# A graph layer on one core: four more units of eight tiles, the left-edge check in another bank, and 14 slots for gathered rows

## The reference

```python
hs = h[src]; hd = h[dst]; e = concatenate([hs, hd], axis=1)
a_k = exp(relu(e @ W_att_k + b_att_k))              # k = 1, 2, 3
att_k = segment_sum(a_k, dst)
avg_a = (a1 / att1[dst] + a2 / att2[dst] + a3 / att3[dst]) / 3.0
m = avg_a * relu(relu(relu(hs @ W_msg_1 + b_msg_1) @ W_msg_2 + b_msg_2) @ W_msg_3 + b_msg_3)
h_neigh = segment_sum(m, dst) / maximum(deg, 1.0)
out = relu(concatenate([h, h_neigh], axis=1) @ W_c1 + b_c1) @ W_c2 + b_c2
x = layernorm(x + out)
```

## Time and profile before

| | us |
|---|---|
| three runs | 770.85, 774.49, 776.41 (median 774.49) |
| the profiled execution | 772.04 |
| its span, first to last instruction | 767.9 |
| granted TensorE clock over the span, share of full | 0.864 |
| PE, DVE, ACT, POOL busy | 651.9, 593.9, 486.6, 553.2 |

### The profile page before, as it was taken

How to read it: one execution, slowest core, us unless ns; L and a number is a source line. 1 busy time by engine, 2 the same in 40 slices (tenths; PEclk the granted TensorE clock), 3 DMA queues, 4 the chain that set the end, 5 groups by cost and what they waited for, 6 DMA issues and landing times.

```text
span 767.9 us, 17623 instructions
## 1 busy us (share of the span) xinstructions
PE 651.9 (85%) x5388; PEld 535.7 (70%) x5388; DVE 593.9 (77%) x1881; ACT 486.6 (63%) x1128; POOL 553.2 (72%) x576
## 2 busy tenths in 40 slices
PE   8962679898879957789999999999988888888785
PEld 5752457765656633469999999999977777777664
DVE  4883577989777969877888888888765778777776
ACT  5554776877665536557777777777565555655563
POOL 7677777777777775467777777777777777777760
PEclk9985597879797776659999999999989788989797
DMA  7984353433883323223333333333352444445431
GB/s 224 258 207 105 67 80 82 97 81 79 77 71 86 67 59 88 46 56 72 82 79 81 79 81 80 82 82 79 76 137 65 107 131 107 118 105 136 101 95 34
DMA packets 81572, 73.70 MB, mean 96 GB/s; under 512 B 34056, under 2 KB 65472, under 8 KB 81472
## 3 DMA queue, kind: packets, MB, share of 16 engines
q0 software_dynamic: 18112, 37.94, 25.3%
q1 hardware_dynamic: 63072, 34.43, 16.8%
q10 hardware_dynamic: 288, 0.13, 0.1%
HBM read 62.91 MB, written 9.52 MB: 94 GB/s over the span
## 4 chain that ended last, share of the span: by engine, by line
PE 43%; POOL 22%; DVE 13%; issue 12%; ACT 6%; DMA 2%; DVEq 1%; SPq 0%; ACTq 0%
POOL work L1428 22%; PE bank L1660 15%; PE bank L1615 9%; PE bank L1641 3%; PE bank L1621 3%; DVE counts L1940 3%; DVE acc L1925 2%; DVE acc L2128 2%; ACT acc L1777 2%; PE bank L646 2%; PE bank L667 2%; PE bank L1567 1%; DMA work<-message_table,src_t 1%; PE bank L655 1%; PE bank L1572 1%
## 5 line engine op out<-in xcount | busy, mean ns | idle before, releaser
L1428 POOL DMA_INDIRECT work<-message_table,src_t x526 | 511.8, 973 | 178.4 <-issue 155.9
L1615 PE MATMUL bank<-work 128*128 128x144 f32 (+7 forms) x1132 | 175.8, 310 | 24.0 <-DVE acc L2128 23.9
L1615 PEld LDWEIGHTS bank<-work 128*128 128x128 f32 x1132 | 163.6, 220 | 33.8 <-issue 19.3
L1803 ACT COPY work<-bank 128x192 f32<-128x192 f32 (+5 forms) x120 | 36.0, 300 | 183.1 <-DVE work L2078 181.0
L2128 DVE TENSOR_TENSOR acc<-acc,bank 128x192 f32 (+7 forms) x283 | 85.9, 303 | 27.0 <-issue 4.4
L1660 PE MATMUL bank<-shared,acc 128*128 128x129 f32 (+1 forms) x784 | 95.6, 275 | 0.0
L2109 DVE TENSOR_TENSOR work<-bank,work 128x576 f32<-128x576 f32 (+5 forms) x120 | 83.5, 696 | 12.5
L1660 PEld LDWEIGHTS bank<-shared,acc 128*128 128x128 f32 (+1 forms) x784 | 91.5, 192 | 0.0
L1641 PE MATMUL bank<-acc 128*128 128x294 bf16 (+3 forms) x240 | 64.4, 406 | 29.6 <-ACT acc L1782 20.9
L1940 DVE TENSOR_TENSOR counts<-counts,bank 128x294 f32 (+3 forms) x120 | 68.9, 574 | 11.4 <-issue 7.5
L1641 PEld LDWEIGHTS bank<-acc 128*128 128x128 bf16 x240 | 23.1, 113 | 69.5 <-ACT acc L1782 36.5
(11 more groups left out here) (188 smaller groups left out, 999.6 us busy)
## 6 DMA issues: line engine op xcount, KB each, us to landing
work<-message_table,src_t POOLq DMA_INDIRECT x526
side<-near_nodes SPq DMA_DIRECT2D x97, 48.0 KB
side<-logit_parts SPq DMA_DIRECT2D x283, 0.8 KB
message_table<-work SPq DMA_DIRECT2D x12, 262.0 KB, 4.5
work<-message_table SPq DMA_DIRECT2D x48, 65.5 KB, 1.8
work<-in_x_t SPq DMA_DIRECT2D x12, 256.0 KB, 4.2
counts<-in_x SPq DMA_DIRECT2D x11, 256.0 KB, 3.4
logits_or_x<-in_x_t SPq DMA_DIRECT2D x11, 256.0 KB
```

Of the source, the lines that this page charges most:

```text
L1428: pool.indirect_dma_start(out=rows_of(n)[:, t, :], out_offset=None, in_=table[:, :], in_offset=bass.IndirectOffsetOnAxis(ap=src_t[:, h, g: ...
L1615: pe.matmul(sums[:, at:at + HEADS * w], rows_here[:, t, 0:P], wt_of(i)[:, t, :], start=h == 0, stop=h == TILES - 1)
```

## The change

`LONG` becomes 26, so units 22 to 25 have eight tiles too: 26 long and 90 short units, 116 in all. The first pass has a ring of 14 slots (`WIDER`) for its first 98 places and of 12 after that; slots 12 and 13 lie in the spare part of plane 3 of `acc`. `FINAL_EVERY` becomes (3, 2): the wide ones begin in steps 81, 83, 86, 88, ..., 101, 103, the next two in 107 and 111. The left-edge check's transpose comes a step later, in step 21, into bank 3, and waits for the early layers' last rows (`s_erow`); the waits of and for the counting bank are gone. Four semaphores are merged with others, whose counts are raised to match.

```diff
-LONG = 22
+LONG = 26
-RING = 12
+RING, WIDER = 12, 14
+WIDER_TO = 7 * WIDER
...
+        more_slots = []
+        for plane, at_slots in ((HEADS, at_spare),):
+            view, _ = spare_area(plane, at_slots, TWO * CHUNK * ROW)
+            more_slots.append(view.rearrange("p (t f) -> p t f", f=ROW))
...
-        LEFT_STEPS, LEFT_PE, LEFT_END = (0, 17, 18, 19), 20, 21
+        LEFT_STEPS, LEFT_PE, LEFT_END = (0, 17, 18, 19), 21, 22
...
-        LEFT_BANK = COUNT_BANKS[LEFT_NEXT % FOUR]
...
-        FINAL_EVERY, FINAL_STEPS = (3, 3), 8
+        FINAL_EVERY, FINAL_STEPS = (3, 2), 8
...
+            def gath_slot(p):
+
+                if not first:
+                    return p % RING
+                return p % WIDER if p < WIDER_TO else (p - WIDER_TO) % RING
+
+            def slot_user(p):
+
+                back = WIDER if first and p < WIDER_TO + RING else RING
+                return max((n for n in range(n_units) if place[n] <= p - back), default=-1)
+
+            def slot_rows(p):
+
+                j = gath_slot(p)
+                if j < RING:
+                    return gath, j * CHUNK
+                return more_slots[(j - RING) // TWO], (j - RING) % TWO * CHUNK
...
+            left_bank = EARLY_BANK if first else SIDE_BANKS[0]
...
                     for n, u in enumerate(order):
-                        if taken(n, RING) >= 0:
-                            pool.wait_ge(s_sum, groups_to(taken(n, RING)))
+                        before = slot_user(place[n] + places[n] - 1)
+                        if before >= 0:
+                            pool.wait_ge(s_sum, groups_to(before))
...
-                                if item == LEFT_NEXT:
-                                    pe.wait_ge(s_left, len(LEFT_STEPS) + 1)
...
                         if i == LEFT_PE:
                             pe.wait_ge(s_left, len(LEFT_STEPS))
                             if first:
-                                pe.wait_ge(s_cadd, LEFT_FREE)
-                            pe.transpose(bank[LEFT_BANK][0:1, 0:P], least[:, :], ident[:, :]).then_inc(s_least, 1)
+                                pe.wait_ge(s_erow, EARLY)
+                            pe.transpose(bank[left_bank][0:1, 0:P], least[:, :], ident[:, :]).then_inc(s_least, 1)
...
-                            act.activation(here, here, ACT.Abs, bias=less_col[0:WIN, 0:1]).then_inc(s_gap, 1)
-                            act.wait_ge(s_gap, before + h + 1)
+                            act.activation(here, here, ACT.Abs, bias=less_col[0:WIN, 0:1]).then_inc(s_hot, 1)
+                            act.wait_ge(s_hot, TWO * (before + h) + 1)
```

More of the change, by code:

```diff
@@ L699, in gnn_program @@
         assert columns_most + UNIT * PARTS <= 512
-        LEFT_STEPS, LEFT_PE, LEFT_END = (0, 17, 18, 19), 20, 21
-        assert LEFT_END < HOT_AT - 4 and LEFT_PE * PAIRS < n_hot
+        LEFT_STEPS, LEFT_PE, LEFT_END = (0, 17, 18, 19), 21, 22
+        assert LEFT_END < HOT_AT - 4 and EARLY_EVERY * EARLY < LEFT_PE
         ONES_AT = max(LEFT_END, early_units[-1])
@@ L799, in gnn_program @@
         s_least = sem("s_least")
-        s_gath = [sem(f"s_gath{j}") for j in range(RING)]
+        s_gath = [sem(f"s_gath{j}") for j in range(WIDER)]
         s_fill = sem("s_fill")
@@ L1271, in taken @@
                 return sum(at < place[i] + places[i] - ring for at in place) - 1
+            def gath_slot(p):
[10 more added lines that the diff above has]
+                return more_slots[(j - RING) // TWO], (j - RING) % TWO * CHUNK
+            assert not first or WIDER_TO <= place[hot_end - TWO]
             def uses(i, ring):
@@ L1311, in early_rows @@
             def early_rows(k):
-                at = (place[early_units[k]] + 1) % RING * CHUNK
-                return gath[:, at:at + CHUNK, 0:P]
+                ring, at = slot_rows(place[early_units[k]] + 1)
+                return ring[:, at:at + CHUNK, 0:P]
             def q_bank(i):
@@ L1333, in rows_of @@
             def rows_of(i):
-                at = place[i] % RING * CHUNK
-                return gath[:, at:at + n_tiles(i), :]
+                ring, at = slot_rows(place[i])
+                return ring[:, at:at + n_tiles(i), :]
             def tiles_at(i, h):
@@ L1345, in rows_landed @@
                         continue
[L1346 removed]
+                    slot = gath_slot(place[i] + h)
                     eng.wait_ge(s_gath[slot], 16 * sum(tiles_at(n, k) for n in range(i + 1) for k in range(places[n])
[L1348 removed]
+                                                       if gath_slot(place[n] + k) == slot))
             def near_of(i):
@@ L1430, in _ @@
                                     in_offset=bass.IndirectOffsetOnAxis(ap=src_t[:, h, g:g + 1], axis=0),
-                                ).then_inc(s_gath[(place[n] + t // CHUNK) % RING], 16)
+                                ).then_inc(s_gath[gath_slot(place[n] + t // CHUNK)], 16)
                     for n in range(n_units - RING, n_units):
@@ L1854, in _ @@
                             for k, a, b in spare_pieces[i - hot_end::ZERO_STEPS]:
-                                act.copy(acc[:, k, a:b], zero_col[:, 0:1].to_broadcast([P, b - a])).then_inc(s_spare, 1)
+                                act.copy(acc[:, k, a:b], zero_col[:, 0:1].to_broadcast([P, b - a])).then_inc(s_zero, 1)
                         for c, step in final_steps(i):
@@ L2062, in another_pass @@
                         dve.wait_ge(s_least, 1)
-                        dve.tensor_reduce(least_all[:, :], bank[LEFT_BANK][0:1, 0:P], AX,
+                        dve.tensor_reduce(least_all[:, :], bank[left_bank][0:1, 0:P], AX,
                                           ALU.min).then_inc(s_left, 1)
@@ L2089, in rows_early @@
                         dve.wait_ge(s_e3, k + 1)
-                        before = max((n for n in range(n_units) if place[n] <= place[early_units[k]] + 1 - RING),
-                                     default=-1)
+                        before = slot_user(place[early_units[k]] + 1)
                         if before >= 0:
@@ L2119, in add_sums @@
                         if first and i == hot_end + ZERO_STEPS:
-                            dve.wait_ge(s_spare, len(spare_pieces))
+                            dve.wait_ge(s_zero, zeroed + len(spare_pieces))
                         for j, g in enumerate(order[i]):
```

18 lines of the change are left out of this document (6 added, 12 removed).

## The result

The kernel after takes 784.7 us (median of four runs, 782.6 to 788.7) against 773.4 us before (four runs, 770.9 to 776.4): a ratio of 1.015, 95% interval 1.010 to 1.021. It is slower by about 11 to 12 us, where I had forecast 9.8 us faster. The profiled execution took 784.9 us, its span is 781.0 us.

The account below looks back on a forecast made before the run. Counting was bound by VectorE and TensorE in turns, hot blocks by TensorE, closings by the compute chain. 6.8 - 3.6 - 11.3 - 5.2 + 3.5 = -9.8 us gave median 764.7 us (profiled 762.2), range 754 to 776.

Parts of the forecast that it names:

- Closings every 3 and 2 units: Closings: five wide ones two units behind the last make VectorE wait 0.7 us each for L971, +3.5 us.
- Rival B: Closings: narrow spacing costs 4.5 us each at TensorE's slower clock, 22.5 us in place of 3.5; 783.7 us, chance 0.09.
- What bounds the kernel now: Whole kernel: counting by VectorE and TensorE in turns, hot blocks by TensorE, closings by the compute chain, not GpSimd.
- rival A: Closings: GpSimd is the bound after all, so all 21.3 us of its stops come back; 753.2 us, chance 0.09.
- Four units of eight tiles: Counting steps: units 22 to 25 get longer and add to the path, +6.8 us, bounds 4.8 to 13.6.
- left-edge check: Counting steps 20 and 21: a later transpose in another bank removes VectorE's idle time, -3.6 us, bounds 0 and -6.6.
- rival C: Counting steps: long units go in series with TensorE's counting, 13.6 not 6.8 us; 773.1 us, no change, chance 0.16.
- Fewer units: Closings: 116 units instead of 120, four fewer at 2.83 us each, -11.3 us, bounds -8.2 and -20.4.
- fourteen slots: Ring: GpSimd no longer stops in counting and hot blocks, so the closings' waits at L2084 go, -5.2 us.

Follow-up runs that it names:

- the rest alone: The kernel after with LONG = 22 and FINAL_EVERY (3, 3) put back, keeping ring of 14, moved check, merged semaphores: 763.8 us, ratio 0.989, then 0.987.

## Why the prediction was wrong

**The step that failed is "Closings every 3 and 2 units".** It put each narrow closing at 0.7 us, from one wait: VectorE's for L969. The runs show 4.1 to 4.8 us: a cycle of 32.1 us where the forecast's own terms give 28.0, 20.6 to 22.6 us for five in the kernel before, and 23.9 us more of VectorE's wait for ScalarE's first copy (29.5 against 5.6). Two things were missing. First, ScalarE's first copy waits not only for L969 but for the one `v_fin` (`s_fr`), and TensorE frees it with L980 of the closing ahead, which in the new order stands behind the block and a whole unit. The wait stands in the listed code (`wide_act`, step 2), and the second pair of order excerpts shows L980 a unit later; I noted the order and did not ask who waits for L980. The second buffer took 14 us away. Second, I took the block near its fast time, 2.94 us; on average it took 3.9 us in the kernel before, with which my own sum gives 1.4 and not 0.7 us. In front of it TensorE waits for VectorE for up to 7 us, and behind that it ran at the slower clock, 4.6 to 5.5 us; without the wait the same 240 instructions took 32.7 us and not 40.4. The same group in the kernel before, from 565 to 722 us:

```profile
L971 PE MATMUL bank<-rest_w,acc 128*128 128x128 f32 x240 | 39.2, 336 | 6.5 <-DVE counts L1133 6.5
```

Its busy time is no less than with two buffers alone (39.2 against 40.4 us), so slow blocks were there before; what the new spacing adds is the wait in front of them (6.5 us here, 26.2 there) and that VectorE has nothing to do beside them. Taking away both brought the kernel from 1.015 to 0.984.

**Rival B** gave 783.7 us, and 784.7 was measured, with 4.5 us for each narrow closing. Its place, price and sign were right; its mechanism only by half, so that it comes within 1 us is in part luck. It has nothing of the one buffer, which made up the larger part (a second one took the wait from 29.5 to 13.5 us), and its own sign did not show: the granted clock of the closings did not fall below 0.85 (0.90 from unit 78 on, 0.88 before), and four blocks of ten were slow, not most of them. It asked for a stretch in which TensorE has already dropped to the slower clock and for a wait for the next unit's products, and set against this that a denser stretch leaves TensorE less idle. It leaves it more idle, 49 us from unit 78 to the last unit where before had 34, of which 24.2 us in front of L969 and 6.5 us in front of L971 (the row above), since TensorE and VectorE take turns there. I gave B a chance of 0.09 and half of that to slower; the range ended at 776 us, below it. Its end on the slow side should have bounded the range, since it was also named as the term's upper bound.

**"What bounds the kernel now" held.** The closings' pace is the compute chain's, not GpSimd's: GpSimd finished 19 us earlier and the kernel later; the rest alone gained 8 to 10 us of the 17 us that GpSimd stopped less; rival A (753 us) is refuted.

**Four units of eight tiles and the left-edge check**, 6.8 - 3.6 = 3.2 us: 4.5 us was measured at the start of the hot blocks. Apart, the check took 4 to 5 us off this stage (3 us of the whole kernel), and the long units added 6.9 us on average, with a scatter from 3.6 to 12.3. On average both sizes are right within 1.5 us; rival C (8.4 us more) did not come.

**Fewer units and fourteen slots**, -11.3 and -5.2 us: the waits at L2084 went, with the ring alone too, where it gave 5 to 7 us. But in the three executions with 26 long units and cheap narrow closings 3.8 to 4.8 us of them are back, nearly all between 575 and 600 us: where the compute chain is fast enough, gathered rows are late again, and little of the -5.2 came there. That the forecast's sum about stands without the failed step is seen where the narrow closings are made cheap: -9.8 us was forecast in all, and the kernel with two buffers and the block later is 9 to 12 us faster than before (0.984 to 0.986). From unit 78 to the last unit, four units fewer with cheap narrow closings take 5 to 9 us off the 193.6 us of the rest; the forecast had -11.3 + 3.5 = -7.8.

**The account.** The profiled execution lies 22.7 us above the forecast's 762.2. Of this 1.3 us are the counting steps, 1.3 us the end behind the last unit (15.5 us against 14.1), and 20.3 us the closings: 205.8 us, where 198.5 - 11.3 - 5.2 + 3.5 = 185.5 were forecast. VectorE's wait for ScalarE's first copy grew by 23.9 us where 3.5 were put, 20.4 us more, which is all of it, if the other two terms are taken as forecast. So that step carries nearly the whole miss.

## What to carry to other kernels

When work is packed closer, list for each moved instruction who waits for the buffer that it frees, not only for what it makes, and follow the first such wait through the queue of the engine that frees it: a buffer that is enough at a distance of three steps may be short at two. A step in an engine's order can undo this with no more work: here the block of products placed one unit later gave back 13 us. And where an upper bound has a price and a place, the range should reach to it, however unlikely it looks.

## What the runs showed of the hardware

Behind waits of 4.3 to 7.2 us TensorE ran the same 24 instructions in 4.6 to 5.5 us, in all eight such blocks of the kernel after and of the one with two buffers, against 2.94 us at best. The granted clock was 0.50 to 0.63 in the slow blocks and 1.00 in those of 2.94 us. Of two blocks behind waits of 2.8 us, one took 2.94 and one 4.57 us, and before, one took 5.38 us behind a wait of only 0.79 us, so the wait ahead is not the only cause. With the waits nearly gone (2.2 us), all 240 of them took 32.7 in place of 40.4 us. A wait in front of a block of products so cost VectorE a second time, behind it. The average granted clock of the whole span does not show where this matters: 0.864 before and 0.875 after, though the kernel after is slower.
